# Two-layer attention and mixture-of-experts kernel: value-pass mask on TensorE, rewritten gates, two-part maxima, one-pass weighted sums, constants made in two portions

## The reference

```
xn = layernorm(x)
x = x + attention0(xn) + moe0(xn)     # 16 heads of 8, causal softmax(q k / sqrt(8)) v, then Wm
xn = layernorm(x)                     # moe0: silu shared expert, 16 experts of 64, top 2
x = x + delta1(xn) + moe1(xn)         # delta1: recurrent state of 8 x 8 per head along the sequence, layernorm, silu gate, Wout
                                      # moe1: 4 of 8 experts of 704 reachable, top 2
```

## Time and profile before

| | us |
|---|---|
| time, median of 3 runs | 1750.98 |
| lowest and highest of them | 1750.64, 1761.45 |
| span of the profiled execution | 1759.6 |
| PE busy | 1587.2 (90%) |
| DVE busy | 1401.9 (80%) |
| ACT busy | 955.8 (54%) |
| POOL busy | 915.0 (52%) |
| mean busy share of the DMA engines, 300 to 600 us | 0.92 to 0.97 |

### The profile page before, as it was taken

How to read it: one execution, slowest core, us unless ns; L and a number is a source line. 1 busy time by engine, 2 the same in 40 slices (tenths; PEclk the granted TensorE clock), 3 DMA queues, 4 the chain that set the end, 5 groups by cost and what they waited for, 6 DMA issues and landing times.

```text
span 1759.6 us, 34071 instructions
## 1 busy us (share of the span) xinstructions
PE 1587.2 (90%) x12430; PEld 1099.6 (62%) x12430; DVE 1401.9 (80%) x2672; ACT 955.8 (54%) x1562; POOL 915.0 (52%) x973
## 2 busy tenths in 40 slices
PE   4899999889899999999989999999999999989950
PEld 2774555555566555445445877788888877778740
DVE  5779877677787878778796998888898899989942
ACT  2741556566666666555743556565555665535620
POOL 5207877651665475678776146622221365654256
PEclk9879999999999999999999999999999999999985
DMA  7963689989999776667448567665666577668413
GB/s 229 303 158 132 186 223 261 273 267 249 283 292 259 214 193 163 153 187 195 119 125 264 165 199 229 195 211 173 192 209 201 185 224 232 189 196 252 132 58 91
DMA packets 277959, 354.69 MB, mean 202 GB/s; under 512 B 32272, under 2 KB 204304, under 8 KB 272416
## 3 DMA queue, kind: packets, MB, share of 16 engines
q1 hardware_dynamic: 237600, 287.92, 57.1%
q0 software_dynamic: 17056, 33.66, 6.9%
q10 hardware_dynamic: 23136, 30.94, 5.1%
HBM read 197.48 MB, written 122.68 MB: 182 GB/s over the span
## 4 chain that ended last, share of the span: by engine, by line
PE 43%; DVE 23%; POOL 9%; issue 9%; DMA 7%; SPq 5%; ACT 4%; ACTq 0%; DVEq 0%; POOLq 0%
PE Y L1124 7%; PE R L867 5%; PE R L900 5%; PE R L869 5%; PE R L868 5%; POOL gat L1408 4%; DVE row_max L1997 3%; POOL xs_dram L1432 3%; DVE state L2098 3%; PE R L883 3%; PE Y L1018 2%; DMA q_rows<-kq 2%; DVE hid L2146 2%; DMA fw<-wf 2%; DVE dw L2092 1%
## 5 line engine op out<-in xcount | busy, mean ns | idle before, releaser
L1432 POOL DMA_INDIRECT xs_dram<-sc_in,pos x256 | 265.1, 1036 | 150.8 <-issue 58.7
L1408 POOL DMA_INDIRECT gat<-ys_dram,pos x256 | 262.6, 1026 | 125.3 <-issue 62.3
L1997 DVE TENSOR_REDUCE row_max<-R 128x6 f32<-128x768 f32 x256 | 238.9, 951 | 63.5 <-PE R L982 58.4
L900 PE MATMUL R<-ident_b 128*128 128x512 bf16 x936 | 255.8, 394 | 32.3 <-DVE K L1850 26.3
L1452 POOL TENSOR_TENSOR o_acc<-o_acc,read 128x512 f32<-128x512 f32 x112 | 146.1, 1304 | 263.8 <-DVE read L2108 262.7
L1124 PEld LDWEIGHTS Y<-fd,hid 128*128 128x128 f32 (+1 forms) x1824 | 232.3, 192 | 53.7 <-DVE hid L2146 25.9
L1604 ACT ACTIVATE probs<-R 128x768 f32<-128x768 f32 x256 | 203.8, 809 | 105.4 <-PE R L1006 99.2
L1124 PE MATMUL Y<-fd,hid 128*128 128x128 f32 (+1 forms) x1824 | 249.9, 280 | 11.3 <-DVE hid L2146 10.7
L1443 POOL TENSOR_SCALAR_AFFINE_SELECT probs<-probs 128x512 f32<-128x512 f32 x256 | 169.8, 664 | 158.1 <-ACT probs L1604 155.1
L867 PE MATMUL R<-fhl,fw 128*128 128x512 f32 x418 | 182.2, 436 | 1.3 <-DVE fhl L2136 1.3
L1723 ACT ACTIVATE sil<-R 128x512 f32<-128x512 f32 x190 | 112.9, 596 | 127.9 <-PE R L869 83.3
(11 more groups left out here) (270 smaller groups left out, 3399.6 us busy)
## 6 DMA issues: line engine op xcount, KB each, us to landing
fw<-wf SPq DMA_DIRECT2D x38, 1408.0 KB, 7.8
q_rows<-kq SPq DMA_DIRECT2D x128, 256.0 KB, 5.1
fx<-xs_dram SPq DMA_DIRECT2D x86, 256.0 KB, 3.4
xs_dram<-gat SPq DMA_DIRECT2D x24, 512.0 KB, 4.9
qk_dram<-qk_parts SPq DMA_DIRECT2D x32, 384.0 KB
Q<-qk_dram SPq DMA_DIRECT2D x64, 192.0 KB
K<-qk_dram SPq DMA_DIRECT2D x64, 192.0 KB
fw<-wf SPq DMA_DIRECT2D x96, 128.0 KB
```

Source lines behind the costliest of these rows:

```text
L900: pe.matmul(psum["R"][:, b * C:(b + 1) * C], ident_b[:, :], ident_b[:, :].unsqueeze(1).to_broadcast([P, TILES, P]), start=True, stop=True)
L1408: pool.indirect_dma_start(gat[:, i % 2, 2 * t + a, :], None, ys_dram[l][g], bass.IndirectOffsetOnAxis(ap=pos[l][g][a][:, col:col + 1], axi ...
L1432: pool.indirect_dma_start(xs_dram[g], bass.IndirectOffsetOnAxis(ap=pos[l][g][a][:, col:col + 1], axis=0), sc_in[:, n % 2, t * P:(t + 1) * ...
L1997: dve.tensor_reduce(row_max[:, b, h2, :, :], pair[:, :].rearrange("p (g c t) -> p g c t", g=2, t=P)[:, :, 0:3, :], AX.X, ALU.max).then_inc ...
```

## The change

It has seven parts.

1. B2 adds the causal mask before the exponential, by a product of all 128 rows for each of the two heads: `causal` as weights, the identity (two times 128 columns) moving. GpSimd's `affine_select` goes, BP waits for ACT alone. GpSimd still waits for each exponential in its list, with nothing to do for it, so that its transfers stay spaced.
2. FU0 writes gate and up projections of a half tile side by side: four products with 64 weight columns in place of two with 128. Tanh and the DVE operations then work on 128 partitions and 256 columns, two DVE operations in place of three.
3. Two bf16 parts of the maxima in place of three, three linked DVE operations in place of seven.
4. The weighted sums (`weigh`) are one product over 128 x 1024 and two additions of 128 x 512 in place of eight operations of 128 x 128.
5. KC is cut in two: KA (nine small operations, all that fillers, A1 and B1 need) comes first, the rest later. `memset` of K goes to GpSimd (KP).
6. C1b additionally waits for the transpose of the chunk before.
7. The planner's lengths and dependences follow; GpSimd's scatters and its gathers of layer 0 are planned at 1.6 us each (`SPACED`) in place of 1.28.

The diff, cut to its core: the planner's entries, then PE (FU0, B2, BP), GpSimd, and DVE (weigh, FU0, BM).

```diff
+ONE_ONE = 1.0 + 16256 / 2.0 ** 23
+SPACED = 1.6
+MAX_PARTS = 2
+ST_ROWS = QK_ROWS + MAX_PARTS
-    stage(12, "KC", early=False, DVE=13.2)
+    stage(5, "KA", early=False, DVE=1.9)
+    stage(45, "KC", early=False, DVE=4.0)
+    stage(17, "KP", early=False, POOL=3.8)
-                stage(t + every * i + every * k / 8, "SC", m, k, after=after, POOL=1.28)
+                stage(t + every * i + every * k / 8, "SC", m, k, after=after, POOL=SPACED)
-            stage(t + 1, "FU0", f, after=[("FT0", f, 0, "ACT")], PE=1.04, ACT=(whole, since(f, 2, ("FD0", 0, "PE"))),
-                  DVE=(1.5, since(f, 2, ("FD0", 0, "PE"))))
+            stage(t + 1, "FU0", f, after=[("FT0", f, 0, "ACT")], PE=1.04, ACT=(0.3, since(f, 2, ("FD0", 0, "PE"))),
+                  DVE=(0.8, since(f, 2, ("FD0", 0, "PE"))))
-                      DVE=(1.5, since(n, 1, ("BM", b, "PE"))), PE=0.25,
+                      DVE=(0.9, since(n, 1, ("BM", b, "PE"))), PE=0.25,
-                stage(t, "B2", n, k, after=[(("BM", n, b, "SP"), 2.4)], PE=0.36,
-                      ACT=(0.7, [("BP", *divmod(i - 2, NPAIR // 2), "PE")] if i >= 2 else []), POOL=0.68)
+                stage(t, "B2", n, k, after=[(("BM", n, b, "SP"), 2.4), ("KC", 0, 0, "DVE")], PE=0.5,
+                      ACT=(0.7, [("BP", *divmod(i - 2, NPAIR // 2), "PE")] if i >= 2 else []), POOL=0.2)
 # PE, FU0
-                    for s in range(2):
-                        to = slice(s * S, (s + 1) * S)
-                        ins = pe.matmul(bank[:, to], fw0[:, n % F0_BUFS, s, 0:2 * F0], fT0[:, par, to], start=True, stop=True)
+                    for i in range(2):
+                        for s in range(2):
+                            ins = pe.matmul(bank[F0 * s:F0 * (s + 1), S * i:S * (i + 1)],
+                                            fw0[:, n % F0_BUFS, s, F0 * i:F0 * (i + 1)],
+                                            fT0[:, par, S * s:S * (s + 1)], start=True, stop=True)
 # PE, B2 (the score products keep their form, with stop=False)
+                    for bank in banks:
+                        ins = pe.matmul(bank[:, 0:2 * P].rearrange("p (c t) -> p c t", t=P), causal[:, :],
+                                        ident_b[:, :].unsqueeze(1).to_broadcast([P, 2, P]),
+                                        start=False, stop=True, skip_group_check=True)
 # PE, BP
-                            wait(*probs_masked(n, 2 * k + c // 2 + 1))
+                            wait(*bank_of["st", n, 2 * k + c // 2].released())
 # GpSimd
+                if kind == "KP":
+                    pool.memset(K[:, :, :, :].rearrange("p n h t -> p (n h t)").bitcast(F32), ONE_ONE).then_inc(k_ones, 1)
+                if kind == "B2":
+                    pool.wait_ge(*bank_of["st", n, k].released())
-                if kind == "B2":
-                    pool.wait_ge(*bank_of["st", n, k].released())
-                    c = 2 * (k % 2)
-                    diag = probs[:, (k // 2) % 2, c:c + 2, 0:2 * P]
-                    pool.affine_select(out=diag, in_=diag, compare_op=ALU.is_ge, fill=0.0, base=0,
-                                       pattern=[[0, 2], [0, 2], [1, P]], channel_multiplier=-1)\
-                        .then_inc(probs_masked.sem, 1)
 # DVE, weigh
+                link(dve.tensor_tensor(rows, rows, shares.unsqueeze(2).to_broadcast([P, 2 * TILES, P]), ALU.mult))
+                pair = rows.rearrange("p (t a) d -> p a t d", a=2)
+                link(dve.tensor_tensor(pair[:, 0], pair[:, 0], pair[:, 1], ALU.add))
+                return dve.tensor_tensor(dst.rearrange(shaped, d=P), pair[:, 0], src.rearrange(shaped, d=P), ALU.add)
 # DVE, FU0
-                    dve.tensor_tensor(lower[:, 0:S], upper[:, 0:S], bank[F0:2 * F0, 0:S], ALU.mult)
-                    dve.tensor_tensor(upper[:, S:C], upper[:, S:C], bank[F0:2 * F0, S:C], ALU.mult).then_inc(bank.free, 1)
+                    dve.tensor_tensor(gated, grown, bank[:, S:C], ALU.mult).then_inc(bank.free, 1)
 # DVE, BM
+                    link(dve.tensor_tensor(peak[:, 1], peak[:, 1], peak[:, 2], ALU.max))
+                    link(dve.tensor_scalar(parts[:, :, 0, :], peak[:, 0:2], -1.0, None, ALU.mult))
+                    dve.scalar_tensor_tensor(out=parts[:, :, 1, :], in0=peak[:, 0:2], scalar=-1.0, in1=parts[:, :, 0, :],
+                                             op0=ALU.mult, op1=ALU.subtract).then_inc(max_split.sem, 1)
```

114 lines of the change are left out of this document (51 added, 63 removed).

## The result

| | before | changed |
|---|---|---|
| time, median of 20 runs each, us | 1751.38 | 1758.36 |
| lowest and highest | 1745.6, 1761.45 | 1747.21, 1767.81 |
| ratio, 95% interval | | 1.0036 [1.0021, 1.005] |

The changed kernel is 7 us slower. That is inside the range of the prediction (1720 to 1778) and within 1%, but on the other side of 1751 than the 1749 forecast. A run's time is its span plus 1.7 us (changed kernel) or 1.9 us (kernel before), so the profiled execution of the kernel before, 1759.6 us long, was a run of about 1761.5 us, 10 us above its own median. The changed kernel's profiled execution, a run of 1757.86 us, is 0.5 us under its median.

What follows compares the result with a forecast made beforehand. PE, executing its list in order with fillers, was taken as the bound until 1700 us; stage terms summed to -2 us, a span of 1757.6 us, less 8.6 us offset a time of 1749 us, 8-in-10 range 1720 to 1778.

Steps and rivals of the forecast that it cites:

- start, to the first router product: Kernel start: early constants and no fillers ahead let the first router product run at about 21 us, -17 us.
- from there to B2: First router product to first B2 step: same work, 145 fillers for 140, +1 us.
- attention (56 + 18 - 60 - 3 - 22): Attention stage, in us: mask products +56, shape changes +18, 277 fillers fewer -60, stages moved out -3, less waiting -22.
- gap (+23 + 4 - 4): Last B2 to layer 1's first expert tile: 105 more fillers +23 us, stages moved in +4, waits gone -4.
- experts of layer 1 (+3 - 1): After the first expert tile: 13 more fillers +3 us, shorter sums -1 us.
- tail: After 1700 us GpSimd's gathers set the end and nothing of the change shortens them, 0 us.
- the start gives nothing: Rival: A-stage chunks wait for transfers on shared DMA engines, +17 us, 1766 us; chance 0.05.
- The offset of 8.6 us: Whole kernel: taken off the summed span because the profiled execution of the kernel before lay that far above the median.
- GpSimd's wait: Attention stage: the value pass's 6.3 us wait for GpSimd's mask goes, counted within the -22 us.
- Waiting melts: Rival: attention waiting falls by 45 us in place of 22 and the start gives 21, 1722 us; chance 0.33.
- Single file: Rival: gate products' column halves do not run side by side, +47 us on PE, 1796 us; 0.11 together with full price.
- The clock falls: Rival: with fewer fillers attention's clock falls to 0.93, 30 us of work left undone, 1779 us; chance 0.09.

Runs made afterwards that it cites:

- before_fourth: The kernel before, unchanged, profiled once more on chip 2; a run of 1750.18 us, median there 1751.62 us.
- after_third: The changed kernel, unchanged, run again on chip 2: 1756.52 us, 1.0022 of the kernel before there.
- start alone: The kernel before with only KC cut in two as in the change (early constants, K filled on GpSimd): 1741.60 us, 0.9918 of the kernel before, chip 7.
- the mask in halves: The changed kernel with B2's mask as four products of 64 rows and 128 columns, same lists: 1744.65 us, 0.9958 of the kernel before, chip 2.
- spaced_128_b: The changed kernel with GpSimd's scatters and gathers of layer 0 planned at 1.28 us, on chip 8: 1891.51 us, 1.0499 of the kernel before.

## Why the prediction was wrong

I compare with before_fourth, a run of 1750.18 us and so 1.2 us from the median, where the first profiled execution was 10 us off. The changed kernel's is 0.5 us off. Their spans differ by 7.7 us, near the 7 us measured. The last column compares two executions on one chip (after_third and before_fourth, chip 2).

| term of the sum | forecast | measured | on chip 2 |
|---|---|---|---|
| start, to the first router product | -17 | -15.1 | -15.2 |
| from there to B2 | +1 | +7.7 | +8.2 |
| attention (56 + 18 - 60 - 3 - 22) | -11 | -17.6 | -24.9 |
| gap (+23 + 4 - 4) | +23 | +26.4 | +29.1 |
| experts of layer 1 (+3 - 1) | +2 | +5.1 | +5.7 |
| tail | 0 | +1.2 | +1.2 |
| sum | -2 | +7.7 | +4.1 |

**The step that failed** is "Between there and the first step of B2 the work is the same and the fillers are 145 for 140: +1 us". It is the largest miss in the direction of the result, 6.7 of the 9.7 us between -2 and +7.7; the smaller ones (start +1.9, gap +3.4, experts +3.1, tail +1.2) are about made up for by attention (-6.6). The work is the same, the time is not: all ten executions with early constants that were not on chip 8 need 123 to 128 us for it, the two of the kernel before 116.7 and 120.5. The early constants alone do it (start alone: 126.9 us). Three parts make up 7.5 us of it: PE idles 13.6 us in place of 10.3 (23 to 148 us after the change, 38 to 155 us in before_fourth); 3.1 us are the products at half pace, which the dropped fillers had absorbed; 1.1 us are the five fillers more. The DMA engines are at 0.82 in place of 0.75. So nearly half of the rival "the start gives nothing" came true; I gave it 0.05. Which of PE, DVE and the transfers lengthens PE's waits there was not tried.

**The offset of 8.6 us.** The execution that the sum was made from was longer than an ordinary one by 10 us, 3.8 us of them in this very stretch, and had 30 us more at half clock. I had the row before me and used it for a rival only. Against that execution the changed kernel's is 3.5 us shorter (1756.1 for 1759.6), which looks like the -2 of the sum. That is luck: a long execution is compared with an ordinary one. The forecast takes the excess off again and so claims -2 us against an ordinary execution, where it is +7.7.

**Right in the mechanism.** A mask product, 0.11 us from start to start, and 0.10 us for a change of shape. The gate products, abreast at 1.01 us; over the whole stage they take 49 to 50 us from start to next start, as before (49). PE's waiting in attention, 34.0 us (727 - 693.0) for 32. DVE's gates, 0.42 us each for 0.42, though its whole fell by 100 us where I had 63 to 70. GpSimd's wait and the tail.

**PE's list in attention, off in its parts.** The forecast makes PE's busy time 11 us longer (56 + 18 - 60 - 3); it became 2 us shorter (695 to 693). This, not a shorter wait, is where the stage gained more than forecast. Counted from start to next start, waits left out, the mask products and the halves ahead of them cost 82 to 83 us more, for 74. The 277 fillers that went were worth 71 to 72 us, 0.26 us each, for 60: I took the pace of a long run (0.218 us), but many stand alone between other products, where the earlier trace rows has 0.32 us. All other products together are some 14 us shorter, for 3.

**Right in size, and in half of the reason.** The gap. PE's fillers did become the last thing that ends: nothing is waited for behind them, and without any transfers the gap is still 74.5 us. Wrong was that GpSimd's transfers follow "in nearly the same sequence, so they would be done no later than before": `rstd` starts 53.6 us after the last B2 step in place of 37.2. Two transfers more ahead of it (14 scatters and 8 gathers for 9 and 11) are 2.5 us of that; the rest is that their long run starts 23.7 us after that step in place of 4.4, behind `o_acc` and `rstd` instructions that wait for DVE. So two chains of nearly the same length end the gap, PE's fillers and GpSimd's list, and cutting the fillers alone gave 5 us. Planning 1.28 shortens both (59 fillers for 218, 11 transfers for 22, the run from 15.5 us on) and gave 30 us in this stretch (73.6 to 43.5).

**Too sure of the bound.** "I therefore add up PE's list" does not hold for attention: without the mask, with the mask in halves and with 51 fillers fewer, 24 of 74, 11 of 46 and none of 11 us came back. That the sum of the attention stage still came within 7 us (14 us on chip 2) is an accident of terms of both signs.

**The rivals.** "Waiting melts": no, 34 us stayed. "Single file": no. "The clock falls": the mean clock is 0.003 lower, which at 1.2 to 1.4 us for each 0.001 goes with about 4 of the 7 us; a seventh of the 30 us that I gave it, but of the right sign. Whether the lower clock causes the longer waits or follows from them was not separated.

## What to carry to other kernels

A length read in one execution carries that execution's clock: look at its mean clock and at where it stood at half, and compare with the other runs' times, before a stage length enters a sum of a few us. Where a planner writes the lists, a planned length that is longer than the real one is a decision on order: look at what stands ahead of the instruction that the next stage waits for, on each engine, and at when that engine gets to it, not only at how much stands in the list. Where two chains end a stretch at nearly the same time, shorten both before you judge either. A kernel that fills its waits is not bound by the full engine alone; take one term away altogether before you price it one to one.

## What the runs showed of the hardware

- One chip of four (chip 8) runs every variant slower, the kernel before by 2.5 to 2.9%, and with late starts of ACT and DVE that go with GpSimd's indirect transfers (29 to 44% against 2 to 6% in the table above). The gain of planning 1.28, 1.6% on chip 7, is a loss of 2.2% there (1.0499 for 1.0275). A version should be measured on more than one chip. The Trainium skill, "SBUF — State Buffer", "SBUF: two separate sides", has a lock between DVE and GpSimd, by which the one that comes second waits for the other's whole instruction, and says that ACT waits for nobody there; ACT starts late on chip 8 as well (29% of 48 exponentials during a transfer in spaced_128_b, 28% of 29 maxima on DVE), so the rule alone doesn't explain it.
- Products at half pace under a view that reads 1.00 (windows of the changed kernel):

```profile
15.00:23.00 8.00, 0.00 (x0) 0.00 (x0) 1.87 (x10) 0.72 (x2) 0.54 (x2) 1.00 1.03 325
23.00:40.00 17.00, 16.71 (x91) 13.61 (x92) 10.90 (x51) 11.80 (x27) 12.27 (x13) 1.00 0.90 305
```

  The trace's records of the granted clock begin at 29.6 us, and the view counts what has no record as 1.00, idle stretches too. At 29.6 us the pace changes as well, from 0.43 us a filler to 0.22. In the first microseconds of a profile the pace of like products tells the clock, not this column. The Trainium skill, "TensorE: Matmul & The Clock Gate", Part 1, has the throttled state as the default that activity ends; the pace from 23.29 us on agrees, as does that of the first fillers of the kernel before (24 take 7.58 us, from 26.33 to 33.91 us, where 24 x 0.218 is 5.2).
- Two DVE operations beside GpSimd's fill of K took 2.1 to 2.2 us in place of 0.69 and 0.17 (as rows of the same lines show right after and before):

```profile
24.23 3.54 POOL L1431 MEMSET K<- 128x4096 f32 x1
```

```profile
22.38 0.17 DVE L1801 TENSOR_SCALAR veps<-mv 128x4 f32<-128x4 f32 x1
...
25.59 2.20 DVE L1801 TENSOR_SCALAR veps<-mv 128x4 f32<-128x4 f32 x1
25.67 2.12 DVE L1873 TENSOR_TENSOR xhl<-R,xhl 128x512 fp32r<-128x512 f32 x1
...
32.31 0.69 DVE L1873 TENSOR_TENSOR xhl<-R,xhl 128x512 fp32r<-128x512 f32 x1 [2.69 <-ACT xhl L1531]
```

  Both ended at 27.79 us, when the fill (24.23 + 3.54 = 27.77) did. The lock of "SBUF: two separate sides" in the Trainium skill holds a DVE operation off for the whole of GpSimd's instruction if it runs in a mode with two ports; the trace agrees as to the ends, and in which mode the `TENSOR_SCALAR` ran no trace shows. It was not in the prediction. PE had no wait in that time, so the fill did hide behind PE, as was said there.
